# The third attention's scan: the first weighing and the maximum change places on VectorE

## The reference

```python
# y[r,c] = x[r,c] * (y[r-1,c-1] + 1) on the lower triangle
a = jnp.einsum('bthd,bshd->bhts', iq, ik)
a = rosa_scan(a.reshape(B * H, T, T)).reshape(B, H, T, T)
a = rosa_attn_score(a, tau)      # x + c/(r+1), mask, softmax(x / tau)
o = jnp.einsum('bhts,bshd->bhtd', a, iv)
o = jnp.einsum('bhtd,hde->bhte', o, xv)
```

## Time and profile before

| stretch of the first group, us | PE busy | DVE busy | ACT busy | POOL busy | PEclk |
|---|---|---|---|---|---|
| 1896 to 2665 (769.00) | 733.69 | 694.62 | 442.96 | 341.05 | 0.98 |
| 2000 to 2180 (180.00) | 165.18 | 160.84 | 117.72 | 106.56 | 1.00 |
| 2190 to 2350 (160.00) | 158.47 | 150.22 | 87.67 | 63.08 | 1.00 |
| 2500 to 2660 (160.00) | 160.00 | 153.46 | 84.02 | 48.49 | 1.00 |

### The profile page before, as it was taken

One profiled execution on the slowest core, in us unless ns is written; L12 is line 12 of the kernel. 1 busy time (PEld: TensorE's weight loads), 2 busy tenths in 40 slices (PEclk: granted clock), 3 DMA queues, 4 the chain that ended last, 5 costly groups with the idle time before them and its releaser, 6 DMA issues. The chain is left out here.

```text
span 3884.8 us, 131167 instructions
## 1 busy us (share of the span) xinstructions
PE 3297.3 (85%) x53977; PEld 2076.2 (53%) x53977; DVE 3089.8 (80%) x7677; ACT 1890.3 (49%) x4422; POOL 1077.7 (28%) x1932
## 2 busy tenths in 40 slices
PE   5999999997778849966689999998689999999329
PEld 1333232231356625643477788875377788877214
DVE  7888788782868845558789999997778999997677
ACT  1666666665345523344466655553366655554200
POOL 1000011100004445430265443322156543332000
PEclk6999999998989969986699999998599999999659
DMA  7023333300010112241000000000000000000128
GB/s 150 18 40 56 57 57 56 57 8 7 0 66 31 35 54 66 69 124 59 8 10 10 9 10 9 9 6 5 6 10 10 10 10 10 9 4 6 52 89 303
DMA packets 104351, 155.92 MB, mean 40 GB/s; under 512 B 17060, under 2 KB 65193, under 8 KB 103728
## 3 DMA queue, kind: packets, MB, share of 16 engines
q1 hardware_dynamic: 90064, 121.41, 12.3%
q0 software_dynamic: 12544, 21.93, 2.0%
q10 hardware_dynamic: 1152, 4.19, 0.3%
HBM read 103.21 MB, written 45.30 MB: 38 GB/s over the span
## 5 line engine op out<-in xcount | busy, mean ns | idle before, releaser
L2081 ACT ACTIVATE s_E<-s_Y,s_M 128x9 f32<-128x9 f32 (+38 forms) x2048 | 656.6, 393 | 626.9 <-DVE s_M L1994 623.7
L365 DVE TENSOR_REDUCE half_max<-shared 128x1 f32<-128x512 f32 x1024 | 644.7, 685 | 84.9 <-PE shared L286 82.1
L1895 PE MATMUL g_x<-s_ik,s_iqm 128*32 128x1 f32 (+63 forms) x16384 | 674.4, 280 | 26.7 <-DVE g_o L1977 11.6
L482 ACT ACTIVATE E<-sc 128x1024 f32<-128x1024 f32 x512 | 496.9, 1021 | 269.8 <-PE sc L300 269.6
L1989 DVE SCALAR_TENSOR_TENSOR s_Y<-s_Y,g_x 128x9 f32<-128x9 f32 (+38 forms) x2048 | 579.3, 283 | 46.7 <-PE g_x L1895 1.2
L1907 PE MATMUL g_p<-mats,s_E 128*128 128x128 f32 x3072 | 449.0, 283 | 41.4 <-ACT s_E L2081 37.5
L1895 PEld LDWEIGHTS g_x<-s_ik,s_iqm 128*32 128x32 f32 x16384 | 393.2, 116 | 153.2 <-issue 77.2
L1907 PEld LDWEIGHTS g_p<-mats,s_E 128*128 128x128 f32 x3072 | 339.6, 144 | 107.5 <-ACT s_E L2081 63.5
L286 PE MATMUL shared<-ks,qs 96*128 96x512 bf16 x1024 | 372.9, 402 | 21.6 <-DVE half_max L365 15.6
L1994 DVE TENSOR_REDUCE s_M<-s_Y 128x4 f32<-128x8 f32 (+56 forms) x512 | 351.2, 686 | 0.2
L2005 DVE TENSOR_TENSOR resid<-g_p,s_W 128x512 f32<-128x512 f32 x384 | 264.0, 687 | 63.2 <-PE g_p L1907 59.2
(11 more groups left out here) (358 smaller groups left out, 5048.3 us busy)
## 6 DMA issues: line engine op xcount, KB each, us to landing
e_spread<-d_gate SPq DMA_DIRECT2D x64, 512.0 KB, 6.1
d_parts<-parts SPq DMA_DIRECT2D x8, 1536.0 KB, 5.9
qs<-d_parts SPq DMA_DIRECT2D x96, 128.0 KB, 8.4
ks<-d_parts SPq DMA_DIRECT2D x96, 128.0 KB, 12.7
me_xg<-d_xs SPq DMA_DIRECT2D x144, 65.0 KB, 1.8
mc_yb<-d_ys SPq DMA_DIRECT2D x8, 1024.0 KB, 8.4
resid<-in_x SPq DMA_DIRECT2D x8, 512.0 KB, 8.2
rden<-d_den POOLq DMA_DIRECT2D x16, 256.0 KB, 3.8
```

Of the source, the lines that this page charges most:

```text
L365: dve.tensor_reduce(half_max[n // SETS % 2][:, idx // 2, idx % 2:idx % 2 + 1], bank("bm", n)[:, :], AX_X, ALU.max).then_inc(max_done, 1)
L482: act.activation(E[:, G % 2, h, :], sc[n % 2][:, :], ACT.Exp, scale=0.25).then_inc(exp_done, 1)
L1895: mm = pe.matmul(x_ps[u % 3][32 * b:32 * (b + 1), rho % 2, 0:n + 1], iqm[n // WINDOW % 2][:, b, x0:x0 + D, :], s.ik[:, b, rho, 0:n + 1], s ...
L2081: act.activation(E[:, m % 2, rho, 0:m + 1], Y[:, D * (m % YR) + rho, 1:2 + m], ACT.Exp, bias=M[:, D - 1 + D * m + rho:D + D * m + rho]).th ...
```

## The change

In each slot of VectorE's loop the order was: step 0, maximum of quad n-1, step 1, first weighing of quad n-2, step 2, (second weighing), step 3. Now it is: step 0, first weighing of quad n-2, step 1, maximum of quad n-1, step 2, (second weighing), step 3. No operation, wait, buffer or other engine's list is changed.

```diff
                     if n < QUADS:
                         recur(n, 0)
+                    if 0 <= n - 2 < QUADS:
+                        weigh(n - 2, 0)
+                    if n < QUADS:
+                        recur(n, 1)
                     if 0 <= n - 1 < QUADS:
                         maximum(n - 1)
-                    if n < QUADS:
-                        recur(n, 1)
-                    if 0 <= n - 2 < QUADS:
-                        weigh(n - 2, 0)
                     if n < QUADS:
                         recur(n, 2)
```

## The result

The changed kernel took 4195.27 us (median of four executions, 4194.6 to 4199.65) against 3885.39 us (3881.85 to 3888.58): a ratio of 1.0796, 95% interval 1.0781 to 1.0812. The forecast was 4208 us. The profiled execution's span is 4193.5 us, 308.7 more than before.

The account below looks back on a forecast made before the run. VectorE and TensorE were taken as nearly full in the scan, VectorE already waiting for turned blocks. A one-slot circle adds 296 us, side work 25: 3886.5 + 321 = 4207.5, say 4208 us; range 4080 to 4290.

Parts of the forecast that it names:

- The circle closes over one slot: Third attention's scan: maximum, exponentials, transposes, weighing and next maximum must fit one slot instead of two; 296 us for both groups.
- Its length: Sum of operations and hand-overs per slot: 2.79, 3.30, 3.85 and 4.40 us in the four stretches from quad 10.
- The start: Before quad 10, at TensorE's 1.2 GHz clock: nine circles of 3.03 us put maximum 10 later by 12.5 us a group.
- Side work: Quotient, rescales and divide per eight-slot chunk not wholly hidden beside the circle: 25 us; rival at 78 us, 4261 us, 8%.
- 0.28 + 0.27: Last quarter, per chunk: TensorE's slot with the quotient exceeds the circle by 0.28 us, VectorE's with the divide by 0.27.
- The clock: Rival: TensorE idles more in the first half and its clock falls, transposes cost 0.46 us more; 4317 us, 8%.
- No change: Rival: VectorE's instructions and waits stay the same in number, so the exchange is free; 3887 us, 5%.
- faster: Rival: from quad 128 step 1 comes up to 0.48 us sooner, so TensorE runs ahead; 3840 us, 3%.
- about 500: Sign in the new profile: first-block weighings wait for transposes about 500 times, several hundred us instead of 94.1.

Follow-up runs that it names:

- maximum ahead: Against the changed kernel, the maximum of quad n-1 moved in front of step 0, the first weighing left behind step 0: 3956.76 us, ratio 1.0179.

## Why the prediction was right

The change did what the argument said at each step:
- *The circle closes over one slot.* The maximum ahead experiment shows it: the same early weighing with a circle over two slots has 98.0 us of waits, not 379.9.
- *Its length.* 2.79, 3.28 and 4.42 measured (the last around quad 225) where 2.79, 3.30 and 4.40 were summed from hand-overs that the trace of before showed at single places. The hand-overs came out the same within 0.01 us, and so one good place for each was enough. The 3.85 of quads 128 to 191 was the mean of two neighbours; slots there without side work took 3.83.
- *The start.* 12.7 against 12.5 us.
- *Side work.* 25 us were taken. It was 19: nothing in the first half, and in the second about 0.7 us a chunk in quads 128 to 191 (250.6 - 64 x 3.83 = 5.5 us over eight chunks) and 0.5 behind them (279.5 - 63 x 4.37 = 4.2). Where it stands can be seen in the timelines of TensorE and of VectorE around the quotient and the divide of one chunk in the last quarter:

```profile
2634.03 0.71 PE L1946 MATMUL g_f<-s_osum,s_wo 128*128 128x128 f32 x4
...
2635.03 1.04 PE L1907 MATMUL g_p<-mats,s_E 128*128 128x128 f32 x8
```

```profile
2631.98 1.04 DVE L1994 TENSOR_REDUCE s_M<-s_Y 128x4 f32<-128x860 f32 x1
...
2635.67 0.69 DVE L2005 TENSOR_TENSOR resid<-g_p,s_W 128x512 f32<-128x512 f32 x1 [0.96 <-PE g_p L1907]
...
2636.56 1.05 DVE L1994 TENSOR_REDUCE s_M<-s_Y 128x4 f32<-128x864 f32 x1
...
2638.70 0.95 DVE L2033 RECIPROCAL s_o<-g_f 128x128 f32<-128x128 f32 x1
...
2639.89 0.37 DVE L1989 SCALAR_TENSOR_TENSOR s_Y<-s_Y,g_x 128x217 f32<-128x217 f32 x1
2640.18 0.68 DVE L2005 TENSOR_TENSOR resid<-g_p,s_W 128x512 f32<-128x512 f32 x1
...
2641.07 1.05 DVE L1994 TENSOR_REDUCE s_M<-s_Y 128x4 f32<-128x868 f32 x1
```

The exponentials of quad 213 had ended at 2634.62, but TensorE was in the quotient and turned only at 2635.03, 0.35 later than it could; the maximum of quad 214 came 4.58 us after that of quad 213 (2636.56 - 2631.98). In the next slot the divide held VectorE until step 0 at 2639.89, and the weighing started at 2640.18, though the turned block had been ready for 0.2 us; 2641.07 - 2636.56 = 4.51. A plain slot there has 4.28 to 4.30. So this chunk pays 0.30 + 0.21 = 0.5 us, where 0.28 + 0.27 were computed. One reading behind the 0.27 was too short: the prediction gave VectorE 2.57 us of work from a maximum to the next weighing, and around quad 225 it is 2688.57 - 0.70 - 2685.06 = 2.81, for the most part because step 0, which needs the step 3 in front of it, starts 0.51 behind it and not 0.29. In plain slots the wait of 0.70 hides that.
- *The clock.* It stayed at 1.00 in the first half, at its level of 2.4 GHz, with TensorE busy 91.14 of 120 us; that rival falls. The Trainium skill (TensorE: Matmul & The Clock Gate, on the HAM clock gate) has the clock released by activity; the trace does not contradict it: TensorE went on working with waits of a fraction of a microsecond between, and the clock stayed granted.
- *No change and faster* fall with 454 waits. For VectorE alone the rule that counts operations and not semaphores (the Trainium skill, VectorE: DVE Perf Modes, Rules for kernel authors) holds nearly, its busy time grew by 25 us; for the kernel it does not, since what changed is who waits for whom. The forecast had "about 500": in some slots a divide or a rescale already holds VectorE until the block is there.

By the spans the forecast was 321 us and the growth 308.7. Of these 12 us about 6 are the circle in the second half, which took 3.83 and 4.37 us a slot without side work where 3.85 and 4.40 stand in the sum; 3 are the side work there, 22 taken and 19 measured; and 3 are the first half, whose side work did not show.

## What to carry to other kernels

When two operations of an in-order engine change places, look for a circle through the other engines that goes from one to the other, and count over how many turns of the loop it closes. An exchange that costs no instruction can halve the number of turns that such a circle has. Its length is the sum of the links and hand-overs, and a turn of the loop can be no shorter than this sum divided by the number of turns, nor than the work of the fullest engine. Here, with one turn, the plain slots came out within 0.03 us of the sum. Take the hand-overs from the places where the receiver already waits.

## What the runs showed of the hardware

- An operation of VectorE that needs the result of its neighbour starts later than one that does not. In the trace with the maximum ahead, around quads 96 to 100, a maximum starts 0.29 us behind the step 3 that it needs; in the kernel before it starts 0.16 behind a step 0 of the same width that it does not need. Three dependent steps of 70 columns cover 0.76 us up to the next operation, where one that is not needed next covers 0.14. It is one of the two costs named for the maximum ahead (67 us).
- VectorE's busy time grew from 3089.8 to 3115.0 us with the same instructions at the same durations. Neighbours that follow each other closely overlap in the trace (a weighing of 0.69 lets the next start after 0.61), and a wait between them ends this overlap; about 330 more waits at 0.08 us would be 26. This is argued, not shown.
- A transpose that comes alone after its wait took 0.33 us from start to end; four in a row took 0.66 together, so each further one adds 0.11.
